# Probabilities times values: 32 queries per stationary piece instead of 64

## The reference

```python
# layer 0 (x normalised, the context is keys and values)
q = (Q @ Wq + bq).reshape(B, S, 16, 8).transpose(0, 2, 1, 3)
k = (K @ Wk + bk) ...   # the same shape
v = (V @ Wv + bv) ...
scores = jnp.einsum('bhqd,bhkd->bhqk', q, k) / jnp.sqrt(jnp.float32(D_K))
...
probs = jax.nn.softmax(scores, axis=-1)
out = jnp.einsum('bhqk,bhkd->bhqd', probs, v)
return out.transpose(0, 2, 1, 3).reshape(B, S, D_MODEL) @ Wo + bo

# layer 1 is the same with one 8x8 weight for all heads, then @ Wo.T + bo
# and in both layers:  x = x + tanh(gate) * attention(layernorm(x), ctx)
#                      x = x + tanh(gate) * experts(layernorm(x))
```

## Time and profile before

| what | us |
|---|---|
| median of 3 runs | 1410.18 |
| lowest, highest | 1409.01, 1416.98 |
| span of the profiled execution, first to last instruction | 1173.7 |
| median less that span: start and end of the launch, which the profile does not show | 236.5 |
| PE busy, share of the span | 1095.9, 93% |
| PEld (weight loads, beside PE) | 930.7, 79% |
| DVE busy | 902.1, 77% |
| ACT busy | 715.9, 61% |
| POOL busy | 543.8, 46% |
| clock granted to TensorE, mean | 0.971 of full |

### The profile page before, as it was taken

How to read it: one execution, slowest core, us unless ns; L and a number is a source line. 1 busy time by engine, 2 the same in 40 slices (tenths; PEclk the granted TensorE clock), 3 DMA queues, 4 the chain that set the end, 5 groups by cost and what they waited for, 6 DMA issues and landing times.

```text
span 1173.7 us, 39887 instructions
## 1 busy us (share of the span) xinstructions
PE 1095.9 (93%) x13589; PEld 930.7 (79%) x13589; DVE 902.1 (77%) x3189; ACT 715.9 (61%) x1565; POOL 543.8 (46%) x699
## 2 busy tenths in 40 slices
PE   6899999999984899999999799999999979999998
PEld 4777777777762899999999577777777768999997
DVE  4778878889887454554543699999999979988886
ACT  4777778777760555555555577777777744444443
POOL 2112565556757334344443866666666421222230
PEclk7999999999996899999999899999999999999999
DMA  7223311111202333333333222222222100000000
GB/s 199 71 79 92 92 56 54 54 55 55 68 29 83 90 94 95 93 96 96 94 95 84 56 50 52 49 48 48 51 50 50 24 2 10 27 18 26 18 18 28
DMA packets 116781, 71.88 MB, mean 61 GB/s; under 512 B 51737, under 2 KB 105241, under 8 KB 116633
## 3 DMA queue, kind: packets, MB, share of 16 engines
q1 hardware_dynamic: 108440, 53.13, 16.8%
q0 software_dynamic: 8192, 16.79, 4.8%
HBM read 45.88 MB, written 22.94 MB: 59 GB/s over the span
## 4 chain that ended last, share of the span: by engine, by line
PE 69%; DVE 8%; ACT 7%; issue 7%; POOL 4%; SPq 2%; DMA 2%; DVEq 0%; ACTq 0%; POOLq 0%
PE ps_m L1741 11%; PE ps_m L1518 8%; PE ps_p L1506 7%; PE ps_s L1468 5%; PE ps_p L1622 5%; PE ps_m L1622 4%; PE ps_s L1478 4%; PE ps_s L1727 3%; PE ps_s L1728 3%; PE ps_s L1729 3%; ACT Kbd L749 3%; PE ps_m L1494 2%; ACT Pr L739 2%; PE ps_s L1610 2%; PE ps_s L1611 2%
## 5 line engine op out<-in xcount | busy, mean ns | idle before, releaser
L970 DVE TENSOR_REDUCE mx<-ps_s 128x8 f32<-128x512 f32 x256 | 168.7, 680 | 36.7 <-PE ps_s L1468 36.3
L1518 PEld LDWEIGHTS ps_m<-Vbd,PT 128*64 128x64 f32 x4096 | 137.8, 138 | 48.4 <-issue 42.8
L709 ACT ACTIVATE PT<-ps_p 128x512 f32<-128x512 f32 x256 | 152.7, 597 | 27.0 <-PE ps_p L1506 24.8
L1518 PE MATMUL ps_m<-Vbd,PT 128*64 128x18 f32 x4096 | 158.2, 213 | 0.2 <-ACT PT L709 0.2
L786 ACT ACTIVATE Kbd<-ps_s,c 128x512 f32<-128x512 f32 x128 | 87.3, 688 | 114.5 <-PE ps_s L1612 114.5
L1506 PE MATMUL ps_p<-cst,Pr 128*128 128x128 f32 x1024 | 155.2, 280 | 0.4 <-DVE orow L1246 0.4
L572 POOL TENSOR_TENSOR spare<-spare 1x1 f32<-1x1 f32 x99 | 21.1, 213 | 285.4 <-DVE b1s L1329 146.0
L648 POOL DMA_INDIRECT w1a<-louts,gi x128 | 125.5, 980 | 38.6 <-issue 29.5
L1741 PE MATMUL ps_m<-xn3T 128*128 128x128 f32 x1136 | 138.0, 275 | 0.2 <-ACT xn3T L851 0.2
L1741 PEld LDWEIGHTS ps_m<-xn3T 128*128 128x128 f32 x1136 | 132.7, 192 | 0.4 <-issue 0.4
L851 ACT ACTIVATE xn3T<-ps_s,b1s 128x256 f32<-128x256 f32 x284 | 111.2, 474 | 26.1 <-PE ps_s L1729 26.0
(11 more groups left out here) (219 smaller groups left out, 2695.8 us busy)
## 6 DMA issues: line engine op xcount, KB each, us to landing
xn3T<-lists SPq DMA_DIRECT2D x71, 128.0 KB, 2.1
louts<-xn3T SPq DMA_DIRECT2D x71, 128.0 KB, 1.9
ctxg<-in_ctxT SPq DMA_DIRECT2D x32, 256.0 KB
Kbd<-in_ctxT SPq DMA_DIRECT2D x512, 8.0 KB
out<-x SPq DMA_DIRECT2D x16, 256.0 KB, 2.3
w1a<-in_L_ffn_W SPq DMA_DIRECT2D x8, 256.0 KB, 3.3
w2a<-in_L_ffn_W SPq DMA_DIRECT2D x8, 256.0 KB, 4.0
Pr<-in_ctxT SPq DMA_DIRECT2D x16, 128.0 KB, 2.4
```

Of the source, the lines that this page charges most:

```text
L709: return nc.scalar.activation(dst, src, ACT.Copy)
L970: V.tensor_reduce(mx[g.par][:, q, :], per_key(ps_s[:, q, :]), AX, ALU.max).then_inc(max_done, 1)
L1518: ins = mm((bank7, bank6)[pr][S * b:S * b + S, VW * j:VW * (j + 1)], PT[c][:, P * i + S * b:P * i + S * b + S], Vbd[g.par][:, 2 * pr + b, ...
```

## The change

The inner loop over two sequences b becomes a loop over four pieces r of 32 queries. Each piece is 32 columns of the stationary operand, its output goes to 32 partitions, and its column tile is 32 wide: columns 0, 32, 64 and 96 of the array. Pieces 0 and 1 multiply the values of sequence 0, pieces 2 and 3 those of sequence 1. Data, sums and places of the result are the same; the semaphore is still given by the last matmul of the call.

```diff
                 for i in range(4):
                     j = 4 * (1 - half) + i
-                    for b in range(2):
-                        ins = mm((bank7, bank6)[pr][S * b:S * b + S, VW * j:VW * (j + 1)],
-                                 PT[c][:, P * i + S * b:P * i + S * b + S], Vbd[g.par][:, 2 * pr + b, j, :],
+                    for r in range(4):
+                        ins = mm((bank7, bank6)[pr][32 * r:32 * r + 32, VW * j:VW * (j + 1)],
+                                 PT[c][:, P * i + 32 * r:P * i + 32 * r + 32], Vbd[g.par][:, 2 * pr + r // 2, j, :],
                                  start=True, stop=True)
                 ins.then_inc(pv_done, 1)
```

## The result

| | us |
|---|---|
| kernel before, median of 4 (lowest, highest) | 1413.58 (1409.01, 1438.71) |
| changed kernel, median of 4 | 1427.05 (1419.45, 1428.38) |
| ratio, 95% interval | 1.0095 (1.0048 to 1.0142) |

What follows compares the result with a forecast made beforehand. Layer 0 was taken as bound by a ring through PE, VectorE and ScalarE, layer 1 by PE with VectorE close behind. Savings of 8.5 + 7.5 = 16 us, 15 kept, gave 1410.2 - 15 = 1395 us; range 1383 to 1414.

Steps and rivals of the forecast that it cites:

- The step that failed: Outside the profiled span of 1173.7 us: the 236.5 us to the timed median were taken as untouched by the change.
- The call on PE: Line 1518 on PE: a call's body falls from 0.47 to 0.27 us; a tile-width change costs 0.10 us.
- The rival of a floor of 25 to 29 ns per matmul: TensorE starts matmuls no faster whatever the tile; a call takes 0.93 us, the kernel 1499 us; chance 0.15.
- Rival B: A tile's 58 ns round on PE does not shrink; a call stays 0.47 us, the kernel takes 1413 us; chance 0.13.
- The sum: Both attention layers together: 8.5 us saved in layer 0 plus 7.5 in layer 1, 16 us, of which 15 kept.
- the slack of `mxl`: Layer 0: PE starts `less_maximum` later than the maxima allow, 0.30 us in the mean, taken as saved over 27 steps.
- the logits' wait: Layer 1: VectorE's only wait in a step, 0.20 us, goes away; 5.4 us over 27 steps.
- Rival C: Layer 1: VectorE is not the limit, so PE's 0.70 us counts in 30 steps; 1381 us; chance 0.10.
- no transfer depends on the change: DMA transfers: none would limit the saving; layer 0's later contexts start earlier by as much as the steps shorten.
- what the prediction named as breaking the sum: Layer 0: VectorE's maxima getting slower would spoil the total saving even with the call right; no size given.
- the saving of calls 0 and 1: Layer 0: these calls ahead of `less_maximum` save 0.40 us together, moving it forward by 0.15 to 0.40 us.
- a ring: Layer 0's 10.10 us step: scores, VectorE's maxima, `less_maximum` on PE, ScalarE without a pause, then the next scores.

Runs made afterwards that it cites:

- the loop: PE's layer-1 steps 4 to 29 as a hardware loop over two steps: 1452.14 us from the kernel before, 1438.25 us from the changed kernel.
- the last experiment: Changed kernel with two of a layer-1 step's four gathers moved in GpSimd's program to the start of the next step: 1442.54 us, ratio 1.0014.

## Why the prediction was wrong

**The step that failed** is the sentence "what lies around the span (236.5 us to the median) has nothing of this change in it". The traces of timed executions have 2 us around the span. The 236.5 us lay inside it, in the attention steps with indirect DMAs, as stalls in which TensorE's matmuls and their signals come late, and as the lower clock behind them. There PE's work is not the steady 183.05 of 183.19 us of the earlier trace rows, and the windows above show what replaces it. Every saving was measured off a timeline that the timed chips do not run.

Under the stall the saving is not just hidden, it is paid back. From the scores' starts in the traces on chips of the first kind (us; besides the two kernels themselves, those with the loop, with plain gathers in layer 1, and that of the last experiment):

| stretch | two tiles | four tiles |
|---|---|---|
| layer 0, groups 7 to 31 | 341.7, 343.4, 353.0 | 325.8, 326.9, 332.8, 337.1, 344.1 |
| layer 1, groups 0 to 31, gathers indirect | 408.6, 417.7 | 422.3, 424.5, 429.6, 429.9 |

Layer 0 is shorter by some 13 us in the mean, layer 1 longer by as much. That layer 1 gets longer because twice as many matmuls of the call have to come while they come late is argued, not shown.

**The call on PE** was right. One call with a width change is 0.38 us (forecast 0.37); two calls are 0.67 us (0.64). Line 1518's PE time is 110.7 us without the stall (125.5 with it); I had said near 100, from the calls' body alone. The rival of a floor of 25 to 29 ns per matmul is refuted: 32 matmuls in 0.38 us are 12 ns each. The Trainium skill, TensorE: Matmul & The Clock Gate, Part 1, has a start-to-start of never under about 25 ns; the trace disagrees with that for matmuls on different column tiles. Rival B is refuted by the same row.

**The sum** of 16 us, kept as 15, is what the kernels without indirect DMAs show: 14.85 us. That it fits so well is luck in part: its two terms were off in opposite directions. From landmarks of their traces (start of the scores of a group), two tiles against four:

| stretch | two tiles | four tiles | difference | forecast |
|---|---|---|---|---|
| layer 0, groups 7 to 31 | 245.35 | 241.61 | -3.7 | -7.2 |
| group 31 to the first of layer 1 | 324.23 | 326.31 | +2.1 | 0 |
| layer 1, groups 0 to 31 | 279.88 | 269.92 | -10.0 | -5.4 to -7.5 |

The rest of the two profiled spans (1173.6 and 1161.3) is at the ends. In layer 0 I gave every step 0.30 us. The scores' starts, two tiles and then four, show which steps have it:

```profile
243.66 1.12 PE L1476 MATMUL ps_s<-Kbd,qT 32*64 32x256 f32 x32 [0.78 <-ACT Vbd L717]
253.76 1.12 PE L1476 MATMUL ps_s<-Kbd,qT 32*64 32x256 f32 x32 [0.77 <-ACT Vbd L717]
264.25 1.12 PE L1476 MATMUL ps_s<-Kbd,qT 32*64 32x256 f32 x32 [0.39 <-DVE rank L1079]
```

```profile
242.18 1.12 PE L1476 MATMUL ps_s<-Kbd,qT 32*64 32x256 f32 x32 [0.92 <-ACT Vbd L717]
251.90 1.12 PE L1476 MATMUL ps_s<-Kbd,qT 32*64 32x256 f32 x32 [0.92 <-ACT Vbd L717]
262.43 1.12 PE L1476 MATMUL ps_s<-Kbd,qT 32*64 32x256 f32 x32 [0.38 <-DVE rank L1079]
```

An ordinary step goes from 10.10 to 9.72 us. The step whose scores wait for VectorE's `rank` goes from 10.49 to 10.53. Of the 24 steps 9 gain the whole 0.38 us, 4 gain 0.28, and 11 gain nothing or next to nothing, one of them getting 0.8 longer. I had averaged the slack of `mxl` over all steps and not asked what else ends them. In layer 1 I had VectorE busy for 8.87 us a step with 0.09 of gaps. The gaps are 0.07, but it is busy 147.87 / 17 = 8.70 us; with two tiles and no indirect DMA it was 149.30 / 17 = 8.78. So the step of 9.11 us loses the 0.20 of the logits' wait as forecast, and 0.08 of busy time and 0.06 of gaps that I had left in; why VectorE's busy time falls is open. Rival C (PE's 0.70 us count in full) is refuted: the step gets 0.34 shorter, and PE's weight loads now wait for VectorE's `On`, `Pr` and `t` in each.

**Where TensorE is not stalled**, on the second kind of chip, the changed kernel gains 0.69%, 7 to 8 us of 1179, not 15. In layer 1 the waits of VectorE between 690 and 940 us say what is in the way; the kernel before, in the profile of the prediction (its columns: us in total, times, longest):

```profile
DVE gl L1097 <- PE ps_s L1572: 4.3, 15, 1.3
DVE x L1133 <- DMA w1a<-louts,gi: 2.2, 4, 0.8
```

the changed kernel on such a chip:

```profile
DVE x L1133 <- DMA w1a<-louts,gi: 5.7, 9, 1.2
DVE gl L1097 <- PE ps_s L1572: 1.1, 3, 0.5
```

The wait for the logits goes from 4.3 to 1.1 us, as forecast, and the wait for the gathered rows takes its place, 2.2 to 5.7 us. My sentence that no transfer depends on the change was wrong here: the gathers have to land within a shorter step. Plain DMAs of the same size never make VectorE wait in that stretch, and the kernel is then at 1160.6 to 1162.2 us.

In layer 0 it is what the prediction named as breaking the sum: VectorE's maxima get slower. Their `mxh` and PE's wait for `mxl`, 101 to 325 us, in the changed kernel and then, on the same chip, with plain scatters:

```profile
L984 DVE CAST mxh<-mx 128x16 fp32r<-128x16 f32 x22 | 9.5, 431 | 0.8
PE ps_s L1478 <- DVE mxl L988: 4.1, 14, 0.8
...
L996 DVE CAST mxh<-mx 128x16 fp32r<-128x16 f32 x22 | 3.8, 175 | 0.8
PE ps_s L1490 <- DVE mxl L1000: 0.3, 1, 0.3
```

The cast takes 431 ns in the mean beside indirect scatters and 175 without (285 in the profile of before). `mxl` comes later by that, `less_maximum` waits for it, and the ordinary step is 10.05 us instead of 9.72. From group 7 to 31 layer 0 takes 245.3 us, as in the profile of before (245.4), and 241.8 with plain scatters. So here the saving of calls 0 and 1 is lost to a slower VectorE. Why the cast is slower is not shown.

**What stays open.** Why one kind of chip lets an indirect DMA hold up TensorE and the other hardly does: four of the chips (1442, 1442, 1417 and 1438 us for the kernel before) are of the one kind and two (1179 us both) of the other, and nothing in a trace tells them apart beforehand. What of GpSimd's work gets in the way is not known either. The Trainium skill, Runtime: NRT & Kernel Launch, Instruction fetch mechanics, has the instruction fetch hidden behind the issue of instructions; nothing here is against that. The stall looks like late instructions, but it stayed in the loop while the instruction queue moved nothing, so for the looped steps at least it is something else. No version that computes the reference and beats both kernels on the first kind of chip was found; gathers with real pauses between them, and moving the routing out of the attention steps, were not tried.

## What to carry to other kernels

Before a profile is trusted, compare its span with the timed median. A gap of 17% is not a launch cost until a trace of a timed execution says so, and it can be some fifteen times the effect that is being forecast. A saving on a ring has to be followed through each kind of step (here 11 of 24 gained nothing), and shorter steps make every transfer that must land within one the next candidate. An edit that is meant to move work in time has to be looked up in the profile before its time is read: a new place in the program can be the old place on the clock. Indirect DMAs on GpSimd beside a TensorE stream of many small matmuls are to be measured against plain DMAs of the same size first: here that was 267 us, the change 15.

## What the runs showed of the hardware that was not expected

- While GpSimd issues indirect DMAs (0.95 us each), TensorE on most chips starts only 5 to 7 matmuls per 0.73 us (32 in 0.38 us otherwise), and VectorE starts 2.6 us after the scores' end; a layer-1 step with four of them is 14 us instead of 8.8, an estimated third of the excess being the lower clock that follows. Plain DMAs on the same queue, with the same packets and bytes, do nothing of the kind; with rows 64 KB apart this was seen on the second kind of chip alone.
- The stall stays when the instruction queue of TensorE's program moves nothing (0 packets in 306 us of looped steps, 14.0 us each).
- On the second kind of chip a small cast of VectorE takes 431 ns beside indirect scatters and 175 without.
- This differs by chip: the kernel before has medians of 1414 to 1443 us on some and 1179 us on others.
- Four column tiles take float32 matmuls of 32 stationary and 18 moving columns at 12 ns each, the width change included; two column tiles of 64 columns took 29 ns.
